# Feature lookup and pairwise dots on one core: eleven looked-up features, one comparison per chunk, pair loads behind stores

## The reference, cut to what matters

```python
e = jnp.stack([tbl_0[ids[:, 0]], ..., tbl_25[ids[:, 25]]], axis=1)
combined = jnp.concatenate([dense[:, None, :], e], axis=1)
z = jnp.concatenate([dense, jnp.einsum('bfd,bgd->bfg', combined, combined)[:, _IU0, _IU1]], axis=1)
h = jnp.concatenate([z, dense], axis=1)
h = jnp.maximum(h @ W_top1 + b_top1, 0.0)
h = jnp.maximum(h @ W_top2 + b_top2, 0.0)
y = h @ W_top3
```

## Time and profile before

| | us |
|---|---|
| median of 3 runs (lowest, highest) | 526.63 (525.46, 535.25) |
| the profiled execution | 522.24 |
| its span, first to last instruction | 520.4 |
| PE, PEld busy | 373.9, 299.5 |
| POOL busy | 352.1 |
| DVE busy | 257.9 |
| ACT busy | 205.5 |

### The profile page before, as it was taken

How to read it: one execution, slowest core, us unless ns; L and a number is a source line. 1 busy time by engine, 2 the same in 40 slices (tenths; PEclk the granted TensorE clock), 3 DMA queues, 4 the chain that set the end, 5 groups by cost and what they waited for, 6 DMA issues and landing times.

```text
span 520.4 us, 8177 instructions
## 1 busy us (share of the span) xinstructions
PE 373.9 (72%) x3360; PEld 299.5 (58%) x3360; DVE 257.9 (50%) x186; ACT 205.5 (39%) x278; POOL 352.1 (68%) x266
## 2 busy tenths in 40 slices
PE   0969689496908450899975782889981937669997
PEld 0758477475807340778854471678851726456887
DVE  5778689483965105659760535649760001102123
ACT  2996945424623123153622425154530314225500
POOL 7888888887888775868887676868887570730000
PEclk9988989797968775799997795799995866779999
DMA  8975746961763513358357353358331520114320
GB/s 197 250 180 153 198 114 182 295 176 42 193 161 108 147 50 90 86 153 210 99 144 193 91 134 95 86 136 219 102 84 50 150 67 6 51 32 108 73 65 10
DMA packets 40327, 64.85 MB, mean 125 GB/s; under 512 B 22013, under 2 KB 22909, under 8 KB 40292
## 3 DMA queue, kind: packets, MB, share of 16 engines
q1 hardware_dynamic: 31152, 47.14, 34.3%
q0 software_dynamic: 8192, 16.79, 12.6%
q10 hardware_dynamic: 948, 0.41, 0.3%
HBM read 54.08 MB, written 10.23 MB: 124 GB/s over the span
## 4 chain that ended last, share of the span: by engine, by line
PE 38%; POOL 24%; issue 15%; another core or an unknown queue 12%; DVE 9%; DMA 1%; ACT 1%; DVEq 0%; ACTq 0%
POOL rows L571 24%; PE look_bank L610 12%; PE short_bank L693 9%; PE out_bank L640 7%; DVE one_hot L901 5%; PE out_bank L654 4%; PE out_bank L649 3%; PE short_bank L678 3%; DVE low_table L888 2%; PE out_bank L666 1%; DMA rows<-in_tbl,all_ids 1%; DVE low_pairs L946 1%; DMA all_ids<-in_ids 0%; DVE low_dense L946 0%
## 5 line engine op out<-in xcount | busy, mean ns | idle before, releaser
L571 POOL DMA_INDIRECT rows<-in_tbl,all_ids x256 | 351.1, 1371 | 109.4 <-issue 75.7
L901 DVE TENSOR_TENSOR one_hot<-spread_ids,chunk_row 128x2048 fp32r<-128x2048 int32 (+2 forms) x82 | 171.2, 2123 | 49.2 <-PE look_bank L610 22.3
L610 PE MATMUL look_bank<-one_hot,high_table 125*128 125x512 f32 x328 | 148.5, 453 | 22.3 <-DVE low_table L888 12.0
L610 PE MATMUL look_bank<-one_hot,low_table 125*128 125x512 f32 x328 | 139.4, 425 | 4.5 <-issue 4.5
L914 DVE COPY all_combined<-short_bank 128x512 f32<-128x512 f32 x32 | 21.7, 690 | 163.9 <-PE short_bank L678 73.3
L610 PEld LDWEIGHTS look_bank<-one_hot,high_table 125*128 125x128 f32 x328 | 69.4, 212 | 44.3 <-DVE low_table L888 12.0
L693 PE MATMUL short_bank<-all_combined 128*59 128x54 f32 x2048 | 71.5, 228 | 23.9 <-issue 22.3
L693 PEld LDWEIGHTS short_bank<-all_combined 128*59 128x59 f32 x2048 | 65.8, 142 | 34.5 <-issue 33.8
L610 PEld LDWEIGHTS look_bank<-one_hot,low_table 125*128 125x128 f32 x328 | 69.1, 211 | 21.8 <-issue 7.5
L678 PE MATMUL short_bank<-identity,rows 128*128 128x128 f32 x256 | 40.0, 303 | 57.8 <-issue 30.1
L678 PEld LDWEIGHTS short_bank<-identity,rows 128*128 128x128 f32 x256 | 31.2, 154 | 63.1 <-issue 57.2
(11 more groups left out here) (41 smaller groups left out, 200.8 us busy)
## 6 DMA issues: line engine op xcount, KB each, us to landing
whole_table<-in_tbl SPq DMA_DIRECT2D x36, 448.0 KB
spread_ids<-in_ids_by_feature SPq DMA_DIRECT2D x40, 256.0 KB
block_scratch<-all_dots SPq DMA_DIRECT2D x24, 208.0 KB
rows<-in_tbl,all_ids POOLq DMA_INDIRECT x256
block_scratch<-all_dots SPq DMA_DIRECT2D x24, 104.0 KB
whole_table<-in_tbl SPq DMA_DIRECT2D x4, 560.0 KB
pairs<-block_scratch SPq DMA_DIRECT2D x72, 29.2 KB
whole_table<-in_tbl SPq DMA_DIRECT2D x36, 52.0 KB
```

Source lines behind the costliest of these rows:

```text
L571: nc.gpsimd.indirect_dma_start(rows[:, t % 2, slot, :], None, tables[ROW_FEATURES[slot]][:, :], bass.IndirectOffsetOnAxis(ap=all_ids[:, t, ...
L610: last = nc.tensor.matmul(look_bank[s % LOOK_BANKS][:], table_parts[part][s % TABLE_PLACES][0:ROWS_K, c, :], one_hot[0:ROWS_K, (chunks_bef ...
L901: last = nc.vector.tensor_tensor(one_hot[:, place:place + n, :], spread_ids[:, s % ID_PLACES:s % ID_PLACES + 1, :].to_broadcast([P, n, COLS]),
```

## The change

Feature 2 (1250 rows) moves from the gathered to the looked-up features: 15 gathers per tile in groups of 4, 4, 4 and 3, and 11 looks per block, two of them of 10 chunks. The ring of one-hots shrinks from 20 to 18 places; that of looked-up vectors has 16 instead of 15 for 11 instead of 10 per block. The halves per tile become 5, 6, 6, 5, the steps of the layers 4, 6, 7, 7. DVE compares one chunk at a time (512 columns). SP issues the pair loads before the first `load_ahead` of the tile.

```diff
-LOOKED_UP = {1: 1000, 5: 1000, 7: 1000, 9: 1000, 17: 1000, 0: 1250, 20: 1000, 22: 1000, 24: 1000, 25: 1000}
+LOOKED_UP = {1: 1000, 5: 1000, 7: 1000, 9: 1000, 17: 1000, 0: 1250, 20: 1000, 22: 1000, 24: 1000, 25: 1000,
+             2: 1250}
...
-HOT_PLACES = 20
+HOT_PLACES = 18
...
-LOOK_PLACES = 15
+LOOK_PLACES = 16
...
-N_GROUPS = N_ROW // IN_GROUP
+N_GROUPS = -(-N_ROW // IN_GROUP)
+GROUP_ROWS = [min(IN_GROUP, N_ROW - g * IN_GROUP) for g in range(N_GROUPS)]
...
-HALVES_AFTER = [6, 5, 5, 4]
+HALVES_AFTER = [5, 6, 6, 5]
+
+OUTS_AFTER = [4, 6, 7, 7]
...
-    outs = out_steps(m - 1)[6 * u:6 * u + 6] if m > 0 else []
+    outs = out_steps(m - 1)[sum(OUTS_AFTER[:u]):sum(OUTS_AFTER[:u + 1])] if m > 0 else []
...
                     store_part(h, range(IN_QUAD // 2) if last else range(IN_QUAD))
-                for s in looks[:1]:
-                    load_ahead(s)
                 for h in ends:
                     if h % 2 == 1 or h >= 2 * LAST:
                         load_part(h, range(IN_QUAD // 2) if last else range(IN_QUAD))
-                for s in looks[1:]:
+                for s in looks:
                     load_ahead(s)
...
-                for q in range(IN_GROUP):
+                for q in range(GROUP_ROWS[g]):
                     last = nc.tensor.transpose(short_bank[g][:, q * P:(q + 1) * P], rows[:, t % 2, g * IN_GROUP + q, :],
                                                identity[:])
+                for q in range(GROUP_ROWS[g], IN_GROUP if t == 0 else 0):
+
+                    last = nc.tensor.transpose(short_bank[g][:, q * P:(q + 1) * P], identity[:], identity[:])
...
-                for c, n, place in runs_of(s, h):
+                for c in halves(s)[h]:
                     last = nc.vector.tensor_tensor(
-                        one_hot[:, place:place + n, :], spread_ids[:, s % ID_PLACES:s % ID_PLACES + 1, :].to_broadcast([P, n, COLS]),
-                        chunk_row[c_all][:, c:c + n].unsqueeze(2).to_broadcast([P, n, COLS]), ALU.is_equal)
+                        one_hot[:, (chunks_before(s) + c) % HOT_PLACES, :], spread_ids[:, s % ID_PLACES, :],
+                        chunk_row[c_all][:, c:c + 1].to_broadcast([P, COLS]), ALU.is_equal)
```

More of the change, by code:

```diff
@@ L390, in group_views @@
             slot = 1 + g * IN_GROUP
-            return (combined[:, :, slot:slot + IN_GROUP],
-                    short_bank[g][:].rearrange("d (s p) -> d p s", s=IN_GROUP))
+            return (combined[:, :, slot:slot + GROUP_ROWS[g]],
+                    short_bank[g][:, 0:GROUP_ROWS[g] * P].rearrange("d (s p) -> d p s", s=GROUP_ROWS[g]))
         def landed(t, g):
-            return gathered[t % 2][g], (t // 2 + 1) * 16 * IN_GROUP
+            return gathered[t % 2][g], (t // 2 + 1) * 16 * GROUP_ROWS[g]
         def part_stored(h):
```

## The result

| | before | after |
|---|---|---|
| median (lowest, highest), us | 526.05 (524.33, 535.25), 4 runs | 548.2 (547.3, 557.61), 4 runs |
| ratio, 95% interval | | 1.0403 (1.0323 to 1.0483): slower |
| profiled execution, its span | 522.24, 520.4 | 548.0, 546.2 |

The account below looks back on a forecast made before the run. It took POOL's gathers, running free while DVE idles and PE trickles, as the main brake. Stage spans 79.4 + 85 + 114 + 111 + 86.5 = 476, with 1.84 around them 478 us; own range 450 to 505, stated range 440 to 530.

Parts of the forecast that it names:

- The gathers' pace: POOL's gathers wait less for shorter DVE comparisons: 1.15 us each, 1.45 with the pause, 21.8 us a tile.
- DVE's work: DVE's busy time per block of four tiles with eleven looks and single-chunk comparisons: 77 us, against 64.57 in tiles 4 to 7.
- loop: DVE runs dry, POOL's gathers run free, PE trickles until they are out, DVE waits for PE; 51 and 43 us excess.
- the term for slow dots: Dot tiles slowed by outlasting gathers: 3.5 us per tile, 14 per block in tiles 4 to 11; bounds 0 and 51.
- rival 1: Fast gathers slow PE whatever DVE does, so every tile's dots wait for its gathers: 520 us; chance 0.12.
- rival 2: DVE's chain starves PE and present slow stretches stay on top of the new work: 554 us, slower; chance 0.16.
- Rival 3: Gathers keep their waits, or PE's slow stretches have nothing to do with POOL: 513 to 521 us; chance 0.10.
- Late ids: Ids behind the moved pair loads reach DVE late: 8 us in tile 3, 5 in tile 7; bounds 0 and 15 each.
- The ring: 18 one-hots instead of 20: no cost while POOL has work during the dots, otherwise one half, 2.4 us, a tile.
- The eleventh look: Ten more chunks per block: PE 83.9 us instead of 79.8; 8 us more show in the start, before tile 0's dots.
- I leave the forecast at 478: Whole-kernel time, unadjusted although the median of three runs, 526.63, lay 4.4 us above the profiled execution.
- the clock: PE's granted clock, 0.82 in tiles 4 to 7, was given a cost of 8 us there.

Follow-up runs that it names:

- a_grouped2: Changed kernel with the comparisons of a half grouped in one instruction again, on chip 8: 510.3 us beside 521.9 for the kernel before, ratio 0.975.
- a_old_sp: Changed kernel with the first look's ids and table issued ahead of the pair loads again, on chip 1: 458.1 us, ratio 0.966.
- b_chunks: Kernel before with one comparison per chunk as its only edit, on chip 1: 412.8 us beside 472.49.
- b_chunks_hot18: Kernel before with one comparison per chunk and a ring of 18 one-hots instead of 20, on chip 6: 414.0 us.
- after_again: Changed kernel run again unedited, on chip 6: 472.5 us, ratio 1.001 to the kernel before.
- a_grouped_old_sp: Changed kernel with grouped comparisons and SP's old order, on chip 6: 471.6 us, ratio 1.000.
- a_grouped: Changed kernel with the comparisons of a half grouped in one instruction again, on chip 1: 472.9 us, ratio 1.000.
- after_third: Changed kernel run once more unedited, on chip 4: 541.7 us beside 521.4 for the kernel before, ratio 1.040.
- b_ids4: Kernel before with one comparison per chunk, 18 one-hots and four places for ids instead of three, on chip 15: 404.3 us, ratio 0.857.
- b_ids4_again: Kernel before with one comparison per chunk, 18 one-hots and four places for ids, repeated on chip 8: 536.7 us, ratio 1.026.

## Why the prediction was wrong

**The gathers' pace: right.** The mean is 1119 ns where 1.15 us was forecast, and a comparison of 512 costs 5.02 / 8 = 0.63 us back to back (0.60 forecast, bounds 0.53 to 0.69).

**DVE's work: right.** 77.74 and 77.58 us of busy time in stages C and D against 77.

**"PE's slow stretches begin when DVE goes idle ... So I take it as a loop": this step failed.** It is the condition of the loop, and with it the term for slow dots. The prediction took the idle DVE as the condition, and so gave nothing in A and B and 3.5 us a tile in C and D. The idle DVE was only what made gathers fast while comparisons were long. With comparisons of one chunk the gathers are fast all the time, and PE creeps with DVE at work (110.34 to 115.18 in tile 1). That the comparisons bring it shows in the edit back: a_grouped2 is at 0.975 of the kernel before on its chip, the changed kernel at 1.040 on chip 4 and in the first pair. Creep beyond the forecast: B 21 us, C 26.5 - 14 = 12.5, D 18 - 14 = 4, E 11.4 - 7.4 = 4, and some 10 in A (16 matmuls in 13.7 us instead of 3.7). That is 51 of the 70 us by which the span missed the forecast (the part of the lower clock in them, 1.7 us in tile 8, included). I read the rest as what waits behind it and did not take it apart. The forecast had this as rival 1, with a chance of 0.12 and a price of 520: the mechanism of rival 1 with nearly the time of rival 2. Its price was too low: 79.4 us for A where 93.0 came, and 340 for B to D (327 and 13 for ids) where 358.6 came. What the earlier trace rows could not tell apart, and the prediction said so, decided the sign.

**Rival 3, and the page behind it.** Gathers did get short and PE's stretches do go with them, so rival 3 falls where the first pair ran. The Trainium skill (SBUF — State Buffer, Who interferes with whom) says that PE never waits on anyone. On chips 1, 6 and 15 the trace agrees (128 matmuls in 3.68 us among gathers 1.25 us apart). On chips 4 and 8 and in the first pair it does not: 14.9 us for the same matmuls. What PE waits for there the profile does not show, so it may be something other than the access to SBUF that the page speaks of.

**Late ids: right in size, for calm chips.** The forecast gave 8 and 5 us for tiles 3 and 7. DVE waits 14.2 us in tile 3 of the first trace:

```profile
189.20 9.36 SPq L531 DMA_DIRECT2D pairs<-block_scratch  x12
198.61 0.47 SPq L480 DMA_DIRECT2D spread_ids<-in_ids_by_feature  x1
```

```profile
203.55 4.91 DVE L906 TENSOR_TENSOR one_hot<-spread_ids,chunk_row 128x512 fp32r<-128x512 int32 x8 [14.17 <-DMA spread_ids<-in_ids_by_feature]
```

and a_old_sp prices the new order at 14.3 us against the forecast's 13. With grouped comparisons the same order costs 1.3, so the agreement holds for single chunks alone.

**The ring: right.** No cost that shows (1.3 us, b_chunks to b_chunks_hot18).

**The eleventh look: mis-sized.** Counted as work: 4.1 us of PE a block and 8 us of stage A. On calm chips it costs 44.1 us once the gathers are out of the way: A 66.6 to 74.2, B 72.8 to 89.0, C 100.2 to 107.4, D 92.0 to 105.3 (b_chunks_hot18 to a_old_sp). The forecast looked for late ids only behind the moved pair loads, not behind the stores of tiles 1, 5 and 9, where six halves now stand instead of five. Those late ids are some 12 us of it, the work of its chunks 10; for the other 22 no run here shows the cause.

**"I leave the forecast at 478".** after_again took 472.5, and its stages C and D, 114.3 and 109.1 us, are the forecast's 114 and 111. That is luck and does not make the forecast right: it was made for a chip on which the kernel before takes 522, and its gain of 44 us was mostly creep taken away, while on chip 6 the kernel before has none and the gain is 0.

**The range and the clock.** The time lies 18 us above the range of 440 to 530, in the direction that had 0.16. The 8 us given to the clock in stage C were not tested: the granted clock there was 0.82 before and 0.84 after. The prediction also read all of tile 12's 12 us as waits. Its first 28 and last 94 matmuls go unbroken in 1.65 and 5.04 us, where 3.68 for 128 gives 3.5; some 3 us of the 12 are the clock, which was 0.50 there.

## What to carry to other kernels

Two engines that contend can protect a third: long DVE instructions held the gathers apart, and that hid a cost that some of these chips have. Before you shorten what holds a stream back, ask what the stream does to others at its full pace, and look whether the trace has a stretch in which it ran so. An edit that frees a resource is worth what the next bound lets through: here the same comparison edit was worth a gain of 59.8 us, of 13.5, nothing (0.5), and a loss of 31, by the number of looks, SP's order and the chip (b_chunks; a_old_sp against a_grouped_old_sp; after_again against a_grouped; after_third against a_grouped2). And a kernel should be timed on several chips: b_ids4 is 14% faster than the kernel before on one kind and 2.6% slower on the other, a_grouped2 2.5% faster on the creeping kind and even on the calm one.

## What the runs showed of the hardware that was not expected

- Two kinds of chip: the same kernel before took 472.5 to 473.1 us on three and 521.9 to 525.8 us on two, one job each, and none was between.
- On the slower kind PE gives groups of one to four small matmuls while gathers follow each other at 1.25 us. The groups mostly start 0.7, 1.4 or 2.1 us apart, and in each of the nine tiles of the first trace 15 to 45 dots go first unbroken, so it looks like something that is used up and then comes in steps; that is a guess. Engines behind PE get its semaphores late: ACT's copy at 120.40 comes after 13.01 us idle, though the 32 matmuls of its fill are among the 37 that the profile ends at 110.01. Look-up matmuls creep too (34.80 to 48.48 in stage A). It stops within some 3 us of the last gather, or, in a_grouped2, some 5 us after the gathers stretch to 2 to 3 us.
- What makes it is open. It is not a full DMA: tile 12 of the kernel before creeps (423.6 to 432.5) at a DMA share of 0.14. It is not a lower clock, as shown above. Nor does the profile show PE waiting for instructions to be loaded: between 101.5 and 121 us of the first trace no queue of the kind "instruction" moved a packet. No kernel here slowed the gathers without changing DVE's work, so that the pace, and not another trait of short comparisons, is the cause rests on a_grouped2's tile 4, on the table of four kernels, and on the creep of the kernel before with DVE idle. That the job and not the chip decides, or that another program on the same chip had a part in it, can't be excluded.
- A gather may wait for more than the running DVE instruction. The prediction bounded the wait by one comparison, 0.6 us. In most places that holds, but in tiles 4 and 8 of the first trace it does not:

```profile
216.66 4.90 DVE L906 TENSOR_TENSOR one_hot<-spread_ids,chunk_row 128x512 fp32r<-128x512 int32 x8
216.67 9.11 POOL L573 DMA_INDIRECT rows<-in_tbl,all_ids  x1 [0.31 <-issue]
...
223.21 1.75 DVE L951 TENSOR_TENSOR low_pairs<-pairs,high_pairs 117x1536 fp32r<-117x1536 f32 x1
```

  The gather begins with the first of eleven DVE instructions that follow each other without a pause, and ends at 225.78, 0.82 us after the last of them. after_again has one of 9.1 us too; in b_ids4_again two such gathers take 18.75 and 17.28 us. When a gather slips in between short instructions and when it does not is open.
